# Finding the tokens of each expert from codes of four tokens, in an expert, attention, expert kernel on one core

## The chip, the cores and the metric

One core of a Trainium2 chip. The metric is the time of one execution on the device in microseconds, as the median of several runs. Engines are named as in the profile: PE is TensorE, DVE VectorE, ACT ScalarE, POOL GpSimd, SP the sync engine that issues most transfers.

## The reference

2,048 tokens of 256 values go through three residual stages: 0.5 of an expert layer, an attention layer, 0.5 of the same expert layer. All is float32.

```python
x = x + 0.5 * moe(layernorm(x))
x = x + attention(layernorm(x))       # 8 sequences of 256, 16 query heads, 4 key/value heads of 128
x = x + 0.5 * moe(layernorm(x))

def moe(x):                            # x: all T = 2048 tokens
    probs = softmax(x @ router_w.T)    # E = 64 experts
    wts, idx = top_k(probs, 8); wts = wts / sum(wts)
    order = argsort(idx.reshape(-1))   # by expert, within one by token
    pos = rank of the assignment within its expert
    valid = pos < 32                   # C = 32: an expert takes its first 32 tokens, the rest is dropped
    h = silu(x[tok] @ w1[e].T) * (x[tok] @ v1[e].T)     # F = 96
    out[tok] += (h @ w2[e]) * wts      # for valid assignments
```

The order of the tokens in an expert layer is position major: token number = 8 * position + sequence. So eight tokens that follow each other are one position of the eight sequences. With 16,384 assignments for 2,048 slots, most are dropped, and each expert keeps the 32 lowest token numbers that chose it.

## The kernel before, in words

**Expert layer** (twice, `expert_layer(0)` and `expert_layer(1)`, each engine has its part). x lies as 16 tiles of 128 tokens. DVE takes mean and variance (`bn_stats`, then `moments`, a row of small dependent operations called levels, each behind a semaphore wait) and writes the normalised tiles xn (L734). PE transposes them (L1139), multiplies with the router (L1117) and transposes back (L1128), ACT copies in between. For each four tiles DVE takes the eight largest logits (MAX8, L769), strikes them out (MATCH_REPLACE, L776) and writes the mask `chosen` (L778).

*Slots.* PE transposes the eight pairs of masks (L1158) into two banks, [expert and half, 512 tokens] each. DVE multiplies by `key_of_column` (L785), which falls with the token number, so that `keys` [128, 1,024] holds one half of the tokens for each expert in 64 partitions and the other half in the other 64. Four rounds of MAX8 (L789) and three of MATCH_REPLACE (L791) give the 32 largest keys, i.e. the lowest token numbers, of each half; both halves are copied side by side (L798, L799), and four more rounds on 64 columns (L801, L804) give the 32 of each expert. PE moves these to [slot, group of four experts] (L1165), DVE turns keys into `slot_index` (L809).

*Weights.* Between the first and second round DVE sums `exp8` and takes 0.5 over the sum (L795 to L797). POOL subtracts the largest logit (L464), ACT takes the exponential (L563), POOL scales (L468) and multiplies by the mask (L472).

*Table.* A table in device memory has one row of 320 values per token: 256 of xn, 64 weights. SP stores xn in eight transfers (L366) and the weights in two (L372). POOL then gathers 128 rows for each of 16 groups of four experts (L484), five in flight, after it has waited for `slot_ready` and for all ten stores:

```python
pool.wait_ge(slot_ready, slot_seen.add(2))
pool.wait_ge(table_written, written.add(160))
for g in range(GROUPS):
    if g >= IN_FLIGHT: ...
    nc.gpsimd.indirect_dma_start(out=slots[:, g % RING, :], ..., in_=table[:, :], ...)
```

*Slot steps* (17 per layer): PE transposes a gathered group (L1027), ACT copies, PE multiplies with the up weights (L1095), ACT and DVE form the gated product, PE transposes it (L1088) and multiplies with the down weights (L1105), ACT and DVE write the weighted result in two parts, and PE adds it into eight-sequence sums by one-hot marks (L1040, L1056).

**What orders the loads.** SP's program is written out by hand. Layer 0: x, small inputs, expert weights of groups 0 to 4 (1.25 MB each), two of the xn stores' four steps, group 5, the other two, groups 6 and 7, the weight stores, a wait for the first three gathers (L392), groups 8 to 11, then the attention weights `wk`, `wq`, `wv` after four slot steps, groups 12 to 15 into buffers as they come free, `wo`. Layer 1: groups 0 to 3 late in the attention; at `attention_done` groups 4 to 11 one behind the other, then the eight xn stores, then the weight stores.

**Attention**: four blocks of 512 tokens, 16 steps each, fp32 products as three fp32r products. DVE's `step` carries chores of block 0 (`in_step`), the late moments of tiles 4 to 15 in steps 8 and 9 among them; `moments(0, 4)` runs before the attention, `moments(0, 12)` before the last output, `moments(12, 16)` after it.

`keep_busy(n)` (L1064) issues n products of 128x128 in fp32 that nobody reads, each as two instructions in the profile.

## Time and profile before

| | us |
|---|---|
| median of 3 runs | 709.76 |
| lowest, highest | 708.30, 709.78 |
| the profiled execution | 710.26 |
| its span, first to last instruction | 708.4 |
| PE, DVE, ACT, POOL busy | 622.9, 509.8, 374.4, 53.8 |

Times in the rows are microseconds from the span's start unless a column says ns. Layer 0 lasts from 0 to about 105 us, the attention to about 606, layer 1 to the end. PE is busiest (88% of the span), but its busy time is no measure inside the expert layers, where it waits and runs at half clock for a part. In windows, PEclk is the granted clock of TensorE (1.00 is 2.4 GHz, 0.50 is 1.2 GHz) and the DMA share is the mean busy share of the core's 16 DMA engines, over 1 where packets overlap. An idle time in brackets names who ended it; "issue" stands for time in which the engine waited for nothing that the profile shows, a transfer's completion among it.

### The profile page before, as it was taken

The page shows a single profiled execution, that of the slowest core. Times are in us where ns is not written, and L with a number is a line of the kernel's source. Part 1 is how long each engine was busy: PE and PEld are TensorE (multiplying, and loading weights), DVE is VectorE, ACT ScalarE, POOL GpSimd, SP SyncE. Part 2 cuts the span into 40 slices and gives each one's busy share as a digit, 9 for nine tenths or more (in the row PEclk, how much of TensorE's full clock was granted, in tenths as well). Part 3 has the DMA queues.
Part 4 walks back from the last instruction along what each step waited for, and adds up shares of the span by engine and source line. Part 5 has one row for each costly group of instructions (what it writes and reads, how often), then busy time and mean ns, then how long its engine had stood idle before and what let it go on. Part 6 is the DMA issues. An engine that isn't in the chain of part 4 may idle for free.

```text
span 708.4 us, 12001 instructions
## 1 busy us (share of the span) xinstructions
PE 622.9 (88%) x4530; PEld 529.1 (75%) x4530; DVE 509.8 (72%) x1289; ACT 374.4 (53%) x1013; POOL 53.8 (8%) x57
## 2 busy tenths in 40 slices
PE   1729988899999999999999999999999998644995
PEld 1406667699988979999897999898799997422774
DVE  6665536688997777778777777876878776893442
ACT  1504534576756655656555656565566565421441
POOL 3153200000000000000000000000000000133310
PEclk9859989999999999999999999999999999875998
DMA  9949960000000000000000000000000042794571
GB/s 329 407 166 393 420 183 2 1 1 1 0 1 2 1 1 1 1 1 1 1 0 1 1 1 1 1 1 1 1 1 1 1 187 111 281 403 124 196 253 47
DMA packets 27133, 62.50 MB, mean 88 GB/s; under 512 B 6880, under 2 KB 17120, under 8 KB 26816
## 3 DMA queue, kind: packets, MB, share of 16 engines
q1 hardware_dynamic: 25008, 55.92, 21.0%
q0 software_dynamic: 1632, 5.38, 2.2%
q8 instruction: 38, 0.62, 0.4%
q10 hardware_dynamic: 432, 0.39, 0.2%
q14 instruction: 23, 0.19, 0.1%
HBM read 54.34 MB, written 7.34 MB: 87 GB/s over the span
## 4 chain that ended last, share of the span: by engine, by line
PE 77%; DVE 12%; DMA 5%; ACT 4%; issue 2%; SPq 0%; POOL 0%; DVEq 0%
PE bank L1214 18%; PE bank L1216 18%; PE bank L1215 18%; PE bank L1266 8%; PE bank L1056 3%; PE bank L1095 3%; DMA down_r<-down_in 3%; PE bank L1105 2%; PE bank L1027 1%; DVE best L789 1%; DVE ln L709 1%; PE bank L1040 1%; DVE keys L791 1%; PE bank L1139 1%; DMA x<-x_in 1%
## 5 line engine op out<-in xcount | busy, mean ns | idle before, releaser
L624 ACT ACTIVATE probs<-bank,negmax 128x256 f32<-128x256 f32 x256 | 121.4, 494 | 0.3 <-DVE negmax L939 0.3
L637 ACT CAST probsT_hi<-bank 128x512 fp32r<-128x512 f32 x128 | 68.9, 590 | 81.0 <-PE bank L1266 81.0
L971 DVE TENSOR_TENSOR probsT_lo<-bank,probsT_hi 128x512 fp32r<-128x512 f32 x128 | 82.0, 683 | 1.4 <-ACT probsT_hi L637 1.4
L939 DVE TENSOR_REDUCE negmax<-bank 128x2 f32<-128x512 f32 x128 | 82.0, 681 | 1.1 <-PE bank L1216 1.1
L607 ACT ACTIVATE o_hi<-bank,bv 128x512 fp32r<-128x512 f32 x64 | 44.2, 690 | 64.9 <-PE bank L1216 64.9
L1214 PE MATMUL bank<-k_hi,q_hi 128*128 128x256 f32 x256 | 72.6, 283 | 2.9 <-DVE q_lo L925 2.9
L947 DVE TENSOR_SCALAR probs<-probs,rowinv 128x256 f32<-128x256 f32 x256 | 73.1, 350 | 2.3
L1214 PE MATMUL bank<-o_hi,wo_hi 128*128 128x256 f32 x256 | 73.1, 286 | 1.6 <-DVE o_lo L925 1.6
L925 DVE SCALAR_TENSOR_TENSOR o_lo<-bank,bv,o_hi 128x512 fp32r<-128x512 f32 x64 | 48.0, 751 | 36.3 <-ACT o_hi L607 36.3
L1216 PE MATMUL bank<-o_hi,wo_lo 128*128 128x256 f32 x256 | 72.5, 283 | 0.0
L1216 PE MATMUL bank<-k_hi,q_lo 128*128 128x256 f32 x256 | 72.5, 283 | 0.0
L1215 PE MATMUL bank<-k_lo,q_hi 128*128 128x256 f32 x256 | 72.4, 283 | 0.0
L1215 PE MATMUL bank<-o_lo,wo_hi 128*128 128x256 f32 x256 | 72.2, 282 | 0.0
L925 DVE SCALAR_TENSOR_TENSOR q_lo<-bank,bq,q_hi 128x512 fp32r<-128x512 f32 x64 | 48.0, 749 | 28.4 <-ACT q_hi L607 28.2
L1266 PE MATMUL bank<-ident,probs 128*128 128x128 f32 x512 | 67.2, 275 | 0.6 <-DVE probs L947 0.6
L1266 PEld LDWEIGHTS bank<-ident,probs 128*128 128x128 f32 x512 | 58.1, 142 | 1.1 <-DVE probs L947 1.1
L624 ACT ACTIVATION_READ_ACCUMULATOR probs<-bank,negmax 128x1 f32 x256 | 57.4, 224 | 0.0
L1214 PE MATMUL bank<-probsT_hi,v_hi 128*128 128x512 f32 x128 | 51.5, 402 | 4.1 <-DVE xT_lo L923 3.2
L1214 PE MATMUL bank<-xT_hi,wq_hi 128*128 128x512 f32 x128 | 54.5, 426 | 0.2 <-DVE k_lo L925 0.2
L1214 PEld LDWEIGHTS bank<-k_hi,q_hi 128*128 128x128 f32 x256 | 48.8, 191 | 6.1 <-DVE q_lo L925 3.7
L607 ACT ACTIVATE q_hi<-bank,bq 128x512 fp32r<-128x512 f32 x64 | 44.8, 700 | 14.7 <-PE bank L1216 14.7
L1214 PEld LDWEIGHTS bank<-o_hi,wo_hi 128*128 128x128 f32 x256 | 48.3, 189 | 4.2 <-DVE o_lo L925 2.0
(165 smaller groups left out, 1318.1 us busy)
## 6 DMA issues: line engine op xcount, KB each, us to landing
up_r<-up_in SPq DMA_DIRECT2D x16, 768.0 KB, 9.3
down_r<-down_in SPq DMA_DIRECT2D x14, 512.0 KB, 10.1
up_q<-up_in SPq DMA_DIRECT2D x8, 768.0 KB, 8.2
up_o<-up_in SPq DMA_DIRECT2D x6, 768.0 KB, 11.9
down_q<-down_in SPq DMA_DIRECT2D x8, 512.0 KB, 9.0
token_table<-xn SPq DMA_DIRECT2D x16, 256.0 KB, 10.0
down_o<-down_in SPq DMA_DIRECT2D x6, 512.0 KB, 13.6
x<-x_in SPq DMA_DIRECT2D x4, 512.0 KB, 5.5
```

Source lines behind the costliest of these rows:

```text
L607: nc.scalar.activation(dst, src, ACT.Identity, bias=bias).then_inc(work_high, 1)
L624: nc.scalar.activation(probs[:, n % 2, t, :], scores_ps[head][:, qt * S:qt * S + S], ACT.Exp, bias=negmax[:, n % 2, t:t + 1], accum_out=ro ...
L637: nc.scalar.copy(probsT[0][:, head].rearrange("p c s -> p (c s)"), probsT_ps[head][:]).then_inc(probsT_high, 1)
L925: nc.vector.scalar_tensor_tensor(lo, src, bias, hi.bitcast(f32), ALU.add, ALU.subtract).then_inc(work_taken, 1)
L939: nc.vector.reduce_max(negmax[:, n % 2, 2 * head:2 * head + 2], scores_ps[head][:].rearrange("p (t s) -> p t s", t=2), AX.X, negate=True). ...
L947: last = nc.vector.tensor_scalar(probs[:, n % 2, t, :], probs[:, n % 2, t, :], rowinv[:, n % 2, t:t + 1], None, ALU.mult)
L971: nc.vector.tensor_tensor(probsT[1][:, head].rearrange("p c s -> p (c s)"), probsT_ps[head][:], probsT[0][:, head].rearrange("p c s -> p ( ...
L1056: last = mm(banks[n][:, D * pair:D * pair + D], marks[:, c:c + P], parts, start=start and pair == 0, stop=stop, skip_group_check=True)
L1214: mm(dst, w[0], m[0], start=start, stop=False, skip_group_check=shared)
L1215: mm(dst, w[0], m[1], start=False, stop=False, skip_group_check=shared)
L1216: return mm(dst, w[1], m[0], start=False, stop=stop, skip_group_check=shared)
L1266: last = nc.tensor.transpose(probsT_ps[head][:, c * S + qt * P:c * S + qt * P + P], probs[:, n % 2, 2 * head + qt, c * P:c * P + P], ident[:])
```

## The change

- **Codes.** ACT writes `code_ident`, four identity matrices scaled by 8, 4, 2, 1 over 32, four copies per expert layer. PE no longer transposes the masks but adds up four scaled transposes in one bank: [expert and half, 256 groups of four tokens], where the value is a code of four bits over 32. Half the partitions hold tokens 0 to 3 of each eight, the other half 4 to 7. DVE adds `key_of_group` to each non-zero code, searches 256 columns instead of 1,024 (`best`), splits rank and code, tests each bit (`part_bits`), gives each of the four tokens its key (`part_keys`), lays both halves side by side as 256 candidates per expert and searches those for the 32 largest.
- **Reciprocal column.** The table's row is 321 values: the 65th weight column is 0.5 over the sum, written by DVE ahead of the key search. POOL's scaling (L468) goes; DVE multiplies by the column in the slot step. POOL's subtraction waits for the masks now; SP's weight store waits for `winv_ready` too.
- **Moments.** 13 levels become 11: two Newton steps for the root in place of three, the first with other constants.
- **Unread products.** 24 on PE at the start, 12 ahead of layer 1, 16 after the move of the slot keys in each layer, ahead of the first gathered group's transposes.
- POOL's setup has six small iotas more, in each layer one iota and cast of 256 columns instead of 1,024.

```diff
-ROW = D + E
+ROW = D + E + 1
...
+KEPT = 0.375
...
+PARTS = B // 2
+GROUPS_OF_TOKENS = T // B
+CODES = 2 * 2 ** PARTS
...
-                chosen = sb(router, "chosen", [P, TILES // 2, 2, E])
-                expw = sb(router, "expw", [P, TILES, E])
+                chosen = sb(router, "chosen", [P, TILES // 2, 2, E], f32r)
+                expw = sb(router, "expw", [P, TILES, E + 1])
...
+                sp.wait_ge(winv_ready, inv_seen.add())
...
+            for n in range(PARTS):
+                nc.gpsimd.iota(bit_of_part[:, n:n + 1], pattern=[[0, 1]], base=2 ** (PARTS - 1 - n),
+                               channel_multiplier=0).then_inc(setup_link, 1)
+            for half in range(2):
+                pool.wait_ge(setup_link, 4 + PARTS + half)
+                nc.gpsimd.iota(part_offset[64 * half:64 * half + 64, :], pattern=[[2, PARTS]], base=2 * PARTS * half,
+                               channel_multiplier=0).then_inc(setup_link, 1)
+            pool.wait_ge(setup_link, 6 + PARTS)
...
-                for half in range(2):
-                    nc.gpsimd.iota(key_i32[64 * half:64 * half + 64, :], pattern=[[-1, 4], [-1024, 2], [-8, P]],
-                                    base=T - 4 * half, channel_multiplier=0).then_inc(key_raw, 1)
-                    pool.wait_ge(key_raw, raw.add())
-                nc.gpsimd.tensor_copy(key_of_column[:], key_i32[:]).then_inc(key_ready, 1)
+                nc.gpsimd.iota(key_i32[:, 0:GROUPS_OF_TOKENS], pattern=[[-2 * B, GROUPS_OF_TOKENS]], base=2 * T,
+                               channel_multiplier=0).then_inc(key_raw, 1)
+                pool.wait_ge(key_raw, raw.add())
+                nc.gpsimd.tensor_copy(key_of_group[:], key_i32[:, 0:GROUPS_OF_TOKENS]).then_inc(key_ready, 1)
 
                 pool.wait_ge(top8_ready, tops.add(4))
-                nc.gpsimd.tensor_tensor(expw[:], logits[:], top8[:, :, 0:1].to_broadcast([P, TILES, E]),
+                pool.wait_ge(chosen_ready, masks.add(4))
+                nc.gpsimd.tensor_tensor(expw[:, :, 0:E], logits[:], top8[:, :, 0:1].to_broadcast([P, TILES, E]),
                                         ALU.subtract).then_inc(shifted, 1)
                 pool.wait_ge(exps, exp_seen.add(2))
-                pool.wait_ge(winv_ready, inv.add())
-                nc.gpsimd.tensor_tensor(expw[:], expw[:], wsum[:, 1, :].unsqueeze(2).to_broadcast([P, TILES, E]),
-                                        ALU.mult).then_inc(scaled_ready, 1)
-                pool.wait_ge(chosen_ready, masks.add(4))
-                pool.wait_ge(scaled_ready, scales.add())
                 nc.gpsimd.tensor_tensor(
-                    expw[:].rearrange("p (h i) e -> p h i e", h=2), expw[:].rearrange("p (h i) e -> p h i e", h=2),
-                    chosen[:].rearrange("p i h e -> p h i e"), ALU.mult).then_inc(weights_ready, 1)
+                    expw[:, :, 0:E].rearrange("p (h i) e -> p h i e", h=2), expw[:, :, 0:E].rearrange("p (h i) e -> p h i e", h=2),
+                    chosen[:].bitcast(f32).rearrange("p i h e -> p h i e"), ALU.mult).then_inc(weights_ready, 1)
...
+                for n in range(PARTS):
+                    nc.scalar.activation(code_ident[:, n, :], ident[:], ACT.Copy,
+                                         scale=2.0 ** (PARTS - 1 - n) / CODES).then_inc(code_ready, 1)
...
-                          (tt, var, stats[:, a:b, 2], stats[:, a:b, 5], ALU.add)],
-                         [(stt, gap2, half_gap, 0.25, half_gap, ALU.mult, ALU.mult), (ts, var, var, 1.0 / D, EPS, ALU.mult, ALU.add),
-                          (ts, mean_, mean_, 0.5, None, ALU.mult)],
-                         [(tt, var, var, gap2, ALU.add)],
+                          (stt, var, stats[:, a:b, 2], EPS * D, stats[:, a:b, 5], ALU.add, ALU.add)],
+                         [(stt, gap2, half_gap, 0.25 / KEPT ** 2, half_gap, ALU.mult, ALU.mult), (ts, mean_, mean_, 0.5, None, ALU.mult)],
+                         [(stt, var, var, 1.0 / D / KEPT ** 2, gap2, ALU.mult, ALU.add)],
 
 
                          [(ts, rstd_.bitcast(i32), var.bitcast(i32), -0.5, ROOT_BITS, ALU.mult, ALU.add)]]
+
                 steps += [[(tt, gap2, rstd_, rstd_, ALU.mult)],
-                          [(stt, gap2, gap2, -0.5, var, ALU.mult, ALU.mult)],
-                          [(stt, rstd_, gap2, 1.5, rstd_, ALU.add, ALU.mult)]] * 3
+                          [(tt, gap2, gap2, var, ALU.mult)],
+                          [(stt, gap2, gap2, -10.0 / 3.0, gap2, ALU.add, ALU.mult)],
+                          [(stt, rstd_, gap2, 5.0, rstd_, ALU.add, ALU.mult)]]
+                steps += [[(tt, gap2, rstd_, rstd_, ALU.mult)],
+                          [(stt, gap2, gap2, -0.5 * KEPT ** 2, var, ALU.mult, ALU.mult)],
+                          [(stt, rstd_, gap2, 1.5, rstd_, ALU.add, ALU.mult)]]
...
-                    tie(nc.vector.tensor_tensor(weight4[:, parity, :], slots[:, u, s + D:ROW:GROUPS], quadrant[:], ALU.mult))
+                    tie(nc.vector.scalar_tensor_tensor(weight4[:, parity, :], slots[:, u, s + D:D + E:GROUPS], slots[:, u, D + E:ROW],
+                                                       quadrant[:], ALU.mult, ALU.mult))
...
+                dve.wait_ge(exps, 2 * layer + 1)
+                tie(nc.vector.tensor_reduce(wsum[:, 0, :], exp8[:], AX.X, ALU.add))
+                tie(nc.vector.reciprocal(wsum[:, 1, :], wsum[:, 0, :]))
+                nc.vector.tensor_scalar(expw[:, :, E], wsum[:, 1, :], 0.5, None, ALU.mult).then_inc(winv_ready, 1)
+
+
+
                 dve.wait_ge(key_ready, key_seen.add())
-                for n in range(2):
-                    dve.wait_ge(chosenT_raw, pairs_seen.add())
-                    last = nc.vector.tensor_tensor(keys[:, 512 * n:512 * n + 512], bank[n][:],
-                                                   key_of_column[:, 512 * n:512 * n + 512], ALU.mult)
-                tie(last)
+                dve.wait_ge(codes_raw, codes_seen.add())
+                codes = bank[0][:, 0:GROUPS_OF_TOKENS]
+                tie(nc.vector.scalar_tensor_tensor(keys[:], codes, 0.0, key_of_group[:], ALU.is_gt, ALU.mult))
+                tie(nc.vector.tensor_tensor(keys[:], keys[:], codes, ALU.add))
                 for n in range(C // 8):
                     tie(nc.vector.max(best[:, 8 * n:8 * n + 8], keys[:]))
                     if n < C // 8 - 1:
                         tie(nc.vector.match_replace(keys[:], best[:, 8 * n:8 * n + 8], keys[:], -1.0))
-                    if n == 0:
-
-                        dve.wait_ge(exps, 2 * layer + 1)
-                        tie(nc.vector.tensor_reduce(wsum[:, 0, :], exp8[:], AX.X, ALU.add))
-                        tie(nc.vector.reciprocal(wsum[:, 1, :], wsum[:, 0, :]))
-                        nc.vector.tensor_scalar(wsum[:, 1, :], wsum[:, 1, :], 0.5, None, ALU.mult).then_inc(winv_ready, 1)
-                nc.vector.tensor_copy(merged[:, 0:C], best[0:E, :])
-                tie(nc.vector.tensor_copy(merged[:, C:2 * C], best[E:P, :]))
+
+                nc.vector.tensor_copy(best_rank[:], best[:])
+                tie(nc.vector.tensor_scalar(best_code[:], best[:], float(CODES), None, ALU.mult))
+                nc.vector.tensor_tensor(part_bits[:], best_code[:].unsqueeze(2).to_broadcast([P, C, PARTS]),
+                                        bit_of_part[:].unsqueeze(1).to_broadcast([P, C, PARTS]), ALU.bitwise_and)
+                tie(nc.vector.tensor_tensor(part_keys[:], best_rank[:].unsqueeze(2).to_broadcast([P, C, PARTS]),
+                                            part_offset[:].unsqueeze(1).to_broadcast([P, C, PARTS]), ALU.subtract))
+                for half in range(2):
+                    rows = slice(E * half, E * half + E)
+                    last = nc.vector.scalar_tensor_tensor(merged[:, half], part_bits[rows], 0.0, part_keys[rows], ALU.is_gt, ALU.mult)
+                tie(last)
+                candidates = merged[:].rearrange("e h c n -> e (h c n)")
                 for n in range(C // 8):
-                    last = nc.vector.max(first_keys(n), merged[:])
+                    last = nc.vector.max(first_keys(n), candidates)
                     if n < C // 8 - 1:
                         tie(last)
-                        tie(nc.vector.match_replace(merged[:], first_keys(n), merged[:], -1.0))
+                        tie(nc.vector.match_replace(candidates, first_keys(n), candidates, -1.0))
...
-                    nc.vector.tensor_scalar(dst[:], bank[4][:, 0:GROUPS], -1.0, float(T), ALU.mult, ALU.add).then_inc(slot_ready, 1)
+                    nc.vector.tensor_scalar(dst[:], bank[4][:, 0:GROUPS], -0.5, float(T), ALU.mult, ALU.add).then_inc(slot_ready, 1)
...
+                pe.wait_ge(code_ready, PARTS * (layer + 1))
                 chosen_seen.add(2)
-                for n in range(2):
+                for m in range(2):
                     pe.wait_ge(chosen_ready, chosen_seen.add())
                     for c in range(4):
-                        last = nc.tensor.transpose(bank[n][:, c * P:c * P + P],
-                                                   chosen[:, 4 * n + c, :, :].rearrange("p h e -> p (h e)"), ident[:])
-                    last.then_inc(chosenT_raw, 1)
+                        part, h = 2 * m + c // 2, c % 2
+                        last = mm(bank[0][:, h * P:h * P + P], chosen[:, 4 * m + c, :, :].rearrange("p h e -> p (h e)"),
+                                  code_ident[:, part, :], start=part == h == 0, stop=part == PARTS - 1, skip_group_check=True)
+                last.then_inc(codes_raw, 1)
...
+                keep_busy(16)
...
+            for _ in range(24):
+                mm(bank[3][:, 0:P], ident[:], ident[:], start=True, stop=True)
...
+            keep_busy(12)
...
```

## Rows read from the trace of the kernel before

**Rows 1.** Chain that ended last, from 0 to 120 us: start, us, what.

```profile
45.78 0.35 PE bank L1165 x8
...
46.70 1.09 POOL slots L484
...
76.41 19.22 DMA down_r<-down_in
...
105.72 0.33 DVE ln L709 x3
...
108.59 1.39 DVE xn L912 x4
```

**Rows 2.** Windows, 56 to 90 us; last come PEclk, DMA share, GB/s.

```profile
56.00:90.00 34.00, 32.85 (x431) 23.37 (x423) 19.50 (x68) 18.73 (x57) 8.79 (x10) 1.00 1.02 416
```

**Rows 3.** Timeline of SyncE's queue, 0 to 110 us: start, us, engine, line.

```profile
41.65 1.34 SPq L372 DMA_DIRECT2D token_table<-expw  x2
52.32 0.33 SPq L357 DMA_DIRECT2D up_o<-up_in  x1
```

**Rows 4.** Chain that ended last, from 560 us on.

```profile
640.45 2.97 issue
```

**Rows 5.** Timeline of SyncE's queue, from 545 us on.

```profile
617.74 17.63 SPq L366 DMA_DIRECT2D token_table<-xn  x8
635.68 2.60 SPq L372 DMA_DIRECT2D token_table<-expw  x2
```

**Rows 6.** Windows, 40 to 41.5 us, columns as in rows 2.

```profile
40.00:41.00 1.00, 0.00 (x0) 0.00 (x0) 0.96 (x3) 0.00 (x0) 1.00 (x1) 0.50 0.12 47
41.00:41.50 0.50, 0.00 (x0) 0.00 (x0) 0.50 (x1) 0.00 (x0) 0.50 (x1) 0.50 0.06 25
```

**Rows 7.** Timeline of DVE, 9 to 58 us.

```profile
30.66 1.12 DVE L778 TENSOR_SCALAR chosen<-struck 128x256 f32<-128x256 f32 x1
...
33.72 1.23 DVE L789 MAX8 best<-keys 128x8 f32<-128x1024 f32 x1
...
35.06 1.21 DVE L791 MATCH_REPLACE8 keys<-best,keys 128x1024 f32<-128x1024 f32 x1
...
43.81 0.22 DVE L801 MAX8 slot_keys<-merged 64x8 f32<-64x64 f32 x1
```

**Rows 8.** Timelines of POOL and of ACT, 0 to 60 us.

```profile
29.61 2.03 POOL L464 TENSOR_TENSOR expw<-logits,top 128x1024 f32<-128x1024 f32 x1 [21.99 <-DVE top L769]
...
39.28 2.35 POOL L472 TENSOR_TENSOR expw<-expw,chosen 128x1024 f32<-128x1024 f32 x1
...
31.67 1.06 ACT L563 ACTIVATE expw<-expw 128x1024 f32<-128x1024 f32 x1 [1.48 <-POOL expw L464]
```

**Rows 9.** DMA, 42.8 to 45.6 us: rate in 40 slices, queue; weight stores' landing.

```profile
GB/s 0 11 154 267 285 293 282 293 285 293 293 293 285 293 286 278 289 293 285 293 282 293 285 293 293 293 285 271 128 22 0 0 0 0 0 0 0 0 0 0
...
q1 hardware_dynamic: 2080, 0.52, 82.8%
...
token_table<-expw SPq DMA_DIRECT2D x2, 256.0 KB, 2.8
```

**Rows 10.** Timeline of DVE, 595 to 656 us.

```profile
604.90 1.28 DVE L956 TENSOR_TENSOR x<-x,bank 128x512 f32<-128x512 f32 x2 [0.97 <-PE bank L1292]
```

**Rows 11.** DMA, 635.5 to 637.5 us: the queue, its packets, MB and share.

```profile
q1 hardware_dynamic: 799, 0.77, 109.4%
```

**Rows 12.** Chain that ended last, from 50 to 120 us.

```profile
51.82 1.44 PE bank L1095 x16
...
56.96 0.79 PE bank L1095 x16
...
113.03 1.50 PE bank L1064 x8
```

**Rows 13.** Timeline of PE, 0 to 54 us.

```profile
32.89 3.31 PE L1070 MATMUL bank<-x,ident 128*64 128x256 f32 x16
...
49.76 0.69 PE L1027 MATMUL bank<-ident,slots 128*128 128x128 f32 x2 [3.67 <-DMA slots<-token_table,slot_index]
```

31 lines of the change are left out of this document (17 added, 14 removed).

## The prediction

> **What bounds the kernel now.** I read the chain of waits first, cut at the two expert layers; between them TensorE carries it and the change touches little. In layer 0 the chain goes through the key search on DVE, which ends just before 45.78, through the gather at 46.70, and then into a transfer that was 19.22 us in the queue, `down_r`, landed at 95.63 [rows 1]. Next, the windows: from 56 to 90 us the DMA engines are busy 1.02 of the time at 416 GB/s [rows 2]. SyncE issues the loads of that stretch from 52.32 on, 5.62 behind the first gather, since it waits for the third to land [rows 3]. So layer 0 ends as early as its first gathers start, and no earlier for a faster TensorE or DVE in the slot steps.
>
> What does the first gather wait for? In layer 1 not for the keys: the slots were ready at 640.45, and 2.97 us of "issue" passed until GpSimd started at 643.42 [rows 4]. It also waits for the ten stores into the token table. SyncE issued the eight token stores over 17.63 us, held up by a full queue, and the two of the weights from 635.68 to 638.28 [rows 5]. This is a DMA backlog that begins with `attention_done`, and the change alters its bytes by four per row. **In layer 1 a shorter search is worth nothing.** In layer 0 the keys came last, but the same bound lies close ahead: the loads of groups 0 to 7 keep the engines full until about 39, and the tail of one or two engines reaches 41.45 (12% of the engines busy in 40 to 41, 6% in the next half microsecond) [rows 6].
>
> **Part 1, the search.** MAX8 takes 1.23 us on 1,024 columns and 0.22 on 64, MATCH_REPLACE 1.21 on 1,024 [rows 7]: 1.05 ns a column, so 0.42 and 0.40 on 256. A round is these two, a value load of 0.09 and the links: 0.97 against 2.58 now. The new timeline of layer 0: the moments give 0.5 (part 3). GpSimd's first product now waits for the masks, so it no more blocks the last of them, which took 1.12 at 30.66 and ended 0.14 behind GpSimd [rows 7, 8]; free, its 256 columns are 0.3 by the slope. It ends at 30.66 + 0.3 - 0.5 = 30.5. But now the scaling of the reciprocals, a tensor_scalar too, stands behind the same GpSimd operation (2.03): 32.7. Two key operations on 256 columns, 0.42 each with links: 33.6. Three rounds and a MAX8: 37.0. The split into parts is new: two short casts of 0.1 to 0.2, two operations of 128 and two of 128 columns on half the partitions, 0.29 each by the slope: 1.4, to 38.4. The second search is three rounds and a MAX8 again, 3.4 (with 64 columns 1.9): 41.8. To the gather it is 0.96, as from 45.74 to 46.70: **42.8 instead of 46.70**. The fp32r products of the codes replace transposes and run beside the sums of exp8: 0. They wait for four ACT copies of 128 columns, issued while ACT waits for TensorE: at worst 1 us on the keys, which 42.8 can bear (below). The short iota and cast on GpSimd lie 20 us ahead of their reader: 0.
>
> **Part 2, the weights.** GpSimd's product no longer needs the scaled one: 30.5 + 2.03, exp 1.06 [rows 8], product 2.35, with handovers 36.1. SyncE is free (its wait for `winv_ready` ends at 32.7), nothing else stands in its queue until the third gather, and the stores queue behind the loads. Alone, the two kept every engine busy for 82.8% of 2.8 us, 2.32 us for 2,080 packets, 18 ns for 256 B; the first bytes came at 42.9 and the second store landed 2.8 behind its issue at 42.99, at 45.8 [rows 3, 9]: 2.9 from first byte to landing. Behind the tail at 41.45 that makes 44.4, and with 0.3 for GpSimd (46.42 to 46.70) the gather goes at 44.7. That is later than 42.8: **the stores are late next**, and the gain is 46.70 - 44.7 = 2.0, not 3.9. The keys have 1.9 of slack.
>
> **Part 3, the moments.** Thirteen levels take 108.59 - 105.72 = 2.87, 0.2 each [rows 1]. Two levels and one operation less are 0.5. The call behind layer 0 pays in full: -0.5. The first call is covered by the backlog, and so is the last (four tiles); the one of twelve tiles ends ahead of DVE's idle 0.97 at 604.90 [rows 10]; the late moments in the attention are shorter by some 0.1 to 0.5 beside TensorE: 0, with -0.5 kept for the range.
>
> **Part 4, rows of 1,284 B.** Rows of 1,280 B start on multiples of 256 B, those of 1,284 do not. No row shows such a packet. Token packets kept the engines busy for 109.4% of 2 us at 799 packets, 44 ns on the mean and 46 for 1,024 B without the few tiny ones [rows 11]; against 18 for 256 B that is 9.3 ns for 256 B more. The lower bound is nothing, the upper one such piece for each packet: 128 packets per engine for the tokens and 128 for the weights, 1.2 us each, 2.4 per layer. I take 0.1 for the tokens, whose source stays as it was, and 0.3 for the weights, whose source and destination both shift: 0.4, near the rows of the same size. It counts in the backlog of either layer. The gathers read offset rows too, 8 per engine each; the 16 in layer 0 lie in the full stretch: +0.1 for all. The third operand in the slot weight: 0, DVE waits for ACT there.
>
> The Trainium skill, "DMA: Bandwidth & Descriptors", section "How a descriptor splits into AXI transactions", speaks against this change: a descriptor that starts off a 256 B boundary begins at the boundary below it, and the bytes ahead of its start cost beats all the same. By it the sum would be that of the first rival.
>
> **Part 5, extra matmuls.** The 24 at the start and the 12 ahead of layer 1 speed up only transposes whose gain the backlog covers: 0; should they end late, it is covered too. The 16 behind the keys: four calls took 1.50 [rows 12], so 6.0. In layer 0 they run from 42.2 to 48.2; the first slots can be taken 3.06 behind the gather [rows 13], at 48.2 with part 4: no delay, and what a warm clock saves there (sixteen matmuls in 1.44 cold, 0.79 warm [rows 12]) goes into the wait for `down_r`. In layer 1, where TensorE is the bound, they start some 4 us before 639.8 and end by 642, about five ahead of the slots; the clock stood at 0.50 in 40 to 41 [rows 6], after idle time since 36.2 [rows 13]. So the slot steps start cold as now: 0.
>
> **Sum** against the profiled execution: gather of layer 0 -2.0 + 0.4, gathers + 0.1, moments - 0.5, layer 1 + 0.4: **-1.6**. It took 710.26 us (span 708.4), 0.5 above the median of 709.76; from the median the forecast is **708.2**.
>
> **Rivals.**
> 1. *Half a piece for every packet.* 4.7 ns on 256 packets per engine, 1.2 per layer: -2.4 + 2.4 = 0.0, 709.8. For it: a packet's time follows its bytes in rows 9 and 11. Against it: nothing in the rows says that skipped bytes are moved. This is what the page's rule does here. Chance 0.26.
> 2. *Slower.* A whole piece or more for every packet, as each touches one block more and memory has to fill partly written blocks: 2.4 per layer, -2.4 + 4.8 = +2.4, 712.2. Its place is the gather of layer 1, which has no reserve: each microsecond of the stores is one of the kernel. It decides from 1.9 per layer. Against it: a 256 B packet pays only 8.7 above its share by bytes. Chance 0.14.
> 3. *The table doesn't bind*, since the tail vanishes and the gather of layer 0 goes by the keys at 42.8: -3.9 - 0.4 = -4.3, 705.5. Or the clock of layer 1 stays up over the gap, which with three cold steps warmed is 2 more than the forecast, 706.2. For it: the tail is one or two engines. Against it: the backlog of layer 1 had such a tail too, and the idle gap. Chance 0.15.
> 4. *The search isn't shorter*: integer operations or casts that cost twice as much, or a longer wait for GpSimd. Up to 1.9 us of that changes nothing, so it is part of the forecast.
>
> The forecast has 0.45. A measurement of this kernel tells 0.2%, 1.4 us, from no change. The forecast's own range is 0 to 0.7 per layer, -2.4 to -1.0, or 707.3 to 708.8; two thirds of it, and rival 3, are faster: 0.48. The rest of it and rival 1 are no change: 0.37. Slower 0.15. The range goes from 705.3, rival 3 with the late moments, to 711.2, and leaves out the full price of rival 2.
>
> **What would show it.** Right: in layer 0 the gather near 45 with the slots ready at about 42.5 and GpSimd idle between; the first loads 5.6 behind it and `down_r` landed 1.6 earlier; in layer 1 the gather 0.4 later behind `attention_done`, with "issue" of 6 us or more ahead of it; packets of the weights at 20 ns, of the tokens at 47. Wrong: a gather in layer 0 right behind the slot index; warm slot steps in layer 1 from the first; packets longer by 9 ns; or a search that lasts beyond 44.

## The result and the profile after

The changed kernel took **715.98 us** (median of 4 runs, 714.54 to 716.52) against 709.03 for the kernel before (707.47 to 709.78): a ratio of **1.0115, 95% interval [1.008, 1.015]**. It is slower by 7 to 8 us, where 708.2 had been predicted, and 715.98 lies far above the range. The profiled execution took 714.54, its span is 712.8.

The chain that ended last in layer 0 (start, us, what):

```profile
42.33 8.60 issue
50.93 1.07 POOL slots L495
...
80.78 19.84 DMA down_r<-down_in
```

And in layer 1, where `attention_done` came at 606.07 (606.29 in the profile of before):

```profile
636.11 12.22 issue
648.33 0.99 POOL slots L495
```

In both layers the slots are ready about 4 us earlier than before (42.33 against 46.42; 30.0 us behind `attention_done` against 34.2), and in both GpSimd starts the gather 4 to 5 us *later* (50.93 against 46.70 [rows 1]; 42.3 behind `attention_done` against 37.1 [rows 4]). "Issue" of 8.60 and 12.22 us stands where the kernel before had 0.3 and 2.97. The keys don't set the gather any more; the ten stores into the table do, and they have become slower. In layer 0 the wait passes on to `down_r`, landed at 100.62 instead of 95.63. That it isn't seen at `attention_done` has its cause between: from DVE's first `xT_lo` on, the attention took 490.2 us in this profile and 493.4 in that of before, near the two ends of what the profiles of all kernels show (490.1 to 493.6).

The search itself, DVE's timeline from 10 to 56 us (start, us, line, operation):

```profile
30.22 0.29 DVE L797 TENSOR_SCALAR chosen<-struck 128x256 fp32r<-128x256 f32 x1
...
31.03 1.61 DVE L804 TENSOR_SCALAR expw<-wsum 128x16 f32<-128x16 f32 x1
32.55 0.41 DVE L811 SCALAR_TENSOR_TENSOR keys<-bank,key_of_group 128x256 f32<-128x256 f32 x1
...
37.70 0.58 DVE L826 SCALAR_TENSOR_TENSOR merged<-part_bits,part_keys 64x128 f32<-64x128 int32 x2
...
42.15 0.17 DVE L838 TENSOR_SCALAR slot_index<-bank 128x16 uint32<-128x16 f32 x1
```

The stores, from POOL's timeline (the product that completes the weights) and from SyncE's queue in both layers:

```profile
33.77 2.16 POOL L483 TENSOR_TENSOR expw<-expw,chosen 128x1024 f32<-128x1024 f32 x1 [1.17 <-DMA token_table<-xn]
```

```profile
35.96 6.27 SPq L382 DMA_DIRECT2D token_table<-expw  x2
...
617.56 18.41 SPq L375 DMA_DIRECT2D token_table<-xn  x8
636.08 2.62 SPq L382 DMA_DIRECT2D token_table<-expw  x2
```

SyncE issues the weights at once, at 35.96, and nothing holds them back but the transfers ahead of them. What they are like on the DMA engines: 44 to 49 us, the rate in 40 slices and the queue (packets, MB, the time they took as a share of 16 engines):

```profile
GB/s 259 255 288 235 237 222 181 206 183 191 189 181 129 85 83 75 94 75 92 69 69 50 85 58 52 31 33 29 25 29 25 17 17 17 6 8 8 12 6 0
...
q1 hardware_dynamic: 1781, 0.49, 81.6%
```

81.6% of 16 engines for 5 us over 1,781 packets is **36.7 ns for 260 B**, where the same working of [rows 9] gave 18 ns for 256 B. Hardly anything else is moving: the packets are slow by themselves. And they are uneven: 30 ns from 44 to 46 us (1,331 packets, 124.5%), 56 ns from 46 to 49 (450 packets, 52.9%). The rate of [rows 9] is a plateau of 290 GB/s that ends within 0.2 us, here it fades over three microseconds, while GpSimd waits for the last of them. The tokens' packets have the same trouble. From 637 to 640 us (the view and columns as before):

```profile
q1 hardware_dynamic: 935, 0.77, 113.5%
```

That is 58 ns a packet on a mean size of 0.77 MB over 935, some 820 B, against 44 for larger ones in [rows 11]. In a stretch with few small ones, 635 to 636 us, it is 51 ns (347 packets, 110.1%), and from 638 to 639 us 68 ns (259, 110.8%). The weights' packets behind them, 640 to 647 us, take 46 ns on the mean (1,966, 80.0%), more than in layer 0.

TensorE's clock in layer 1, in windows (length, busy time of PE, PEld, DVE, ACT, POOL; then PEclk, DMA share, GB/s):

```profile
640.00:642.00 2.00, 1.54 (x14) 1.35 (x13) 0.00 (x0) 0.00 (x0) 0.00 (x0) 1.00 1.28 158
642.00:644.00 2.00, 0.00 (x0) 0.00 (x0) 0.00 (x0) 0.00 (x0) 0.00 (x0) 1.00 1.23 91
644.00:646.00 2.00, 0.00 (x0) 0.00 (x0) 0.00 (x0) 0.00 (x0) 0.00 (x0) 1.00 0.25 21
646.00:648.00 2.00, 0.00 (x0) 0.00 (x0) 0.00 (x0) 0.00 (x0) 0.00 (x0) 0.69 0.04 2
648.00:650.00 2.00, 0.00 (x0) 0.00 (x0) 0.00 (x0) 0.00 (x0) 1.37 (x2) 0.50 0.00 0
```

The unread products end in 640 to 642; TensorE idles from there, and the granted clock is back at 0.50 before the first gather has landed.

### The profile page after: what moved, and what is told of

Read it like the earlier page. It is cut to its first block, busy times and chain, and to the rows that moved or that the text cites. A ratio compares the mean times of both kernels' runs of the same rounds, so it can differ in the third digit from the quotient of the medians.

```text
span 712.8 us, 12276 instructions
## 1 busy us (share of the span) xinstructions
PE 637.2 (89%) x4666; PEld 543.8 (76%) x4666; DVE 502.7 (71%) x1282; ACT 375.7 (53%) x1021; POOL 45.5 (6%) x59
## 4 chain that ended last, share of the span: by engine, by line
PE 73%; DVE 10%; DMA 5%; ACT 5%; issue 4%; POOL 1%; SPq 1%; DVEq 0%; ACTq 0%
PE bank L1248 18%; PE bank L1249 17%; PE bank L1250 17%; PE bank L1300 7%; PE bank L1085 3%; DMA down_r<-down_in 3%; PE bank L1124 3%; PE bank L1134 2%; DMA slots<-token_table,slot_index 2%; PE bank L1069 1%; PE bank L1056 1%; DMA x<-x_in 1%; PE bank L1168 1%; PE bank L1146 1%; POOL slots L495 1%
```

## The experiments

Fifteen kernels ran, in four batches (e1 to e4, e5 to e8, e9 to e12, e13 to e15), each beside 21 to 29 runs of the kernel before, whose medians there were 706.8 to 707.4 us. For each, three times that carry the argument are read from its trace: the gather of layer 0; the gather of layer 1 behind `attention_done` (in brackets the slot index, behind the same event); and the rest, from that gather to the end of the span. Each kernel ran 4 to 12 times; the rows "before" and "after" are those of the first comparison, and each row's three times come from one profile.

| kernel | row, B | ratio to before [95%] | gather 0 | gather 1 (slots 1) | rest |
|---|---|---|---|---|---|
| before | 1,280 | 1 | 46.70 | 37.1 (34.2) | 65.0 |
| after | 1,284 | 1.0115 [1.008, 1.015] | 50.93 | 42.3 (30.0) | 64.5 |
| e1 before, wide row | 1,284 | 1.0182 [1.0142, 1.0223] | 51.26 | 42.2 (34.7) | 65.3 |
| e2 codes, no column | 1,280 | 0.9994 [0.9974, 1.0013] | 45.67 | 37.3 (31.1) | 65.2 |
| e13 e2, shifted source | 1,280 | 0.9982 [0.996, 1.0003] | 45.83 | 37.1 (30.9) | 65.4 |
| e3 | 1,344 | 1.0012 [0.9998, 1.0026] | 46.52 | 38.3 (30.0) | 66.0 |
| e4 | 1,312 | 1.0026 [1.0, 1.0052] | 46.51 | 38.9 (30.0) | 66.8 |
| e12 | 1,296 | 1.0013 [0.9993, 1.0032] | 47.64 | 39.2 (30.0) | 64.3 |
| e14 | 1,288 | 1.0093 [1.0064, 1.0122] | 48.78 | 41.0 (30.0) | 65.1 |
| e5 before, stores earlier | 1,280 | 1.0005 [0.9973, 1.0037] | 46.51 | 34.4 (34.2) | 67.7 |
| e10 e5, loads held | 1,280 | 0.9992 [0.9973, 1.0011] | 46.36 | 34.9 (34.7) | 65.0 |
| e6 e2, stores earlier | 1,280 | 0.9898 [0.9857, 0.994] | 46.12 | 31.8 (31.1) | 67.2 |
| e7 e6, layer 0 too | 1,280 | 0.9902 [0.9875, 0.993] | 44.64 | 32.1 (31.1) | 65.5 |
| e8 e7, no unread products | 1,280 | 0.9928 [0.99, 0.9956] | 44.04 | 32.0 (31.7) | 67.9 |
| **e9 e7, loads held** | 1,280 | **0.9873 [0.9848, 0.9899]** | 43.51 | 32.0 (31.1) | 64.0 |
| e11 after, as e9 | 1,284 | 1.0027 [1.0011, 1.0042] | 49.31 | 37.3 (30.0) | 65.0 |
| e15 e12, as e9 | 1,296 | 0.9946 [0.9926, 0.9965] | 44.58 | 34.1 (30.0) | 68.0 |

**Is it the row?** e1 is the kernel before with nothing but a column of zeros behind the weights, which nobody uses:

```diff
-ROW = D + E
+ROW = D + E + 1
...
+                nc.gpsimd.memset(expw[:, :, E:E + 1], 0.0).then_inc(key_raw, 1)
```

> The kernel before with one column more in the table's row (zeros, stored and gathered, read by nobody): rows of 1,284 B, weight packets of 260 B, all else as before. Theory (the offset rows make the stores slow): layer 1's gather starts 5 us later behind attention_done than before's 37.1, weight packets take 30 to 45 ns on the mean and token packets 55 to 70, and the whole is 714 to 718 us. Rival A (the cost of the change lies in its other parts: codes, split, unread products): the gather stays where it was and the time is 709 to 710.

It measured 1.0182 [1.0142, 1.0223], 718.81 us: the slowest kernel of all, and just above the 714 to 718 I had named. Its chain in layer 1:

```profile
643.67 7.48 issue
651.15 1.02 POOL slots L486
```

The gather is 5.1 us later than in the kernel before, as expected. Token packets take 52 ns from 638 to 639 us (344 packets, 111.5%) and 65 from 640 to 641 (277, 112.5%). Weight packets take 35 ns in layer 0 (44.5 to 50 us: 1,698, 67.3%) and 48 in layer 1 (643 to 650: 2,019, 85.9%), the latter above the 45 that I had named.

e2 is the other half of that test, the whole change without the column (GpSimd's scaling is back):

```diff
-ROW = D + E + 1
+ROW = D + E
...
+                pool.wait_ge(winv_ready, inv.add())
+                nc.gpsimd.tensor_tensor(expw[:], expw[:], wsum[:, 1, :].unsqueeze(2).to_broadcast([P, TILES, E]),
+                                        ALU.mult).then_inc(scaled_ready, 1)
```

> The changed kernel with the reciprocal column alone undone: rows of 1,280 B again, GpSimd scales by the reciprocals again (1.9 us more ahead of the weight stores); codes, moments, unread products stay. Theory: layer 1's gather at 37 behind attention_done, layer 0's at 44.5 to 46, packets of 18 and 46 ns, 706 to 709.5 us. Rival A: 714 to 716, little changed.

It measured 0.9994 [0.9974, 1.0013]; its chain at the gathers of both layers:

```profile
42.06 3.61 issue
45.67 1.09 POOL slots L500
...
633.00 6.17 issue
639.16 1.00 POOL slots L500
```

So the column carries the whole loss, 1.0115 over 0.9994 or **1.2%, 8.6 us** (in the kernel before 1.8%; why it is more there isn't shown), and everything else in the change together is worth nothing that can be told from zero. The two traces split it: layer 0's gather is 5.3 us later with the column, of which 4.2 are left at `attention_done`; layer 1's is 5.0 later; behind it 0.8 come back; in sum 8.4, the difference of the spans, 712.8 - 704.4.

**Which offsets?** e3, e4, e12 and e14 are the changed kernel with columns of zeros behind the reciprocal one, up to 80, 72, 68 and 66 in all, which GpSimd sets early; in e3 and e4 `held_token` lies in the place of `slot_weight`, to make room:

```diff
-ROW = D + E + 1
+WIDTH = 80
+ROW = D + WIDTH
```

> The changed kernel with 15 zeros behind the reciprocal column: rows of 1,344 B, that is 21 times 64 B but off the 256 B grid in three of four rows, weight packets of 320 B. Theory, if what costs is a partly written piece of 64 B or less: token packets back at 46 ns, weights at 20 to 21, layer 1's gather 37.5 behind attention_done, 706.5 to 710 us. Rival B (any start off a 256 B boundary costs): token packets stay at 53 ns or more, 712 to 716 us.

> As the one of 1,344 B with 7 zeros: rows of 1,312 B, 41 times 32 B, weight packets of 288 B. If the piece is 32 B: packets at 46 and 20 ns and 706.5 to 710 us as with 1,344. If it is 64 B: half of the rows are written in part, packets between those of 1,344 and of 1,284, 710 to 714 us. If 256 B: 712 to 716.

> The changed kernel with three columns of zeros behind the reciprocal column: rows of 1,296 B, which start on multiples of 16 B but not of 32, and weight packets of 272 B. Rows of 1,312 B (multiples of 32) gave 1.0026 with the gather of layer 1 at 38.9 us behind attention_done, rows of 1,284 B gave 1.0115 with 42.3. Theory (memory is written in units of 32 B and a part of one costs): as 1,284, the gather at 41 to 42.5 and the ratio at 1.009 to 1.012. Rival (the unit is 16 B or less, what hurts are offsets of 4 B): as 1,312, the gather at 38.5 to 39.5 and the ratio at 1.002 to 1.004.

> The changed kernel with one column of zeros behind the reciprocal column: rows of 1,288 B, on multiples of 8 B. Rows of 1,284 B gave the gather of layer 1 at 42.3 us behind attention_done, those of 1,296 B 39.2. Theory (the unit is 16 B): as 1,284, gather at 41.5 to 43, ratio 1.009 to 1.013. Rival (only odd multiples of 4 B cost): as 1,296, gather at 38.5 to 39.5, ratio 1.001 to 1.004.

"Issue" ahead of layer 1's gather was 8.27 us in e3, 9.20 in e12 and 10.93 in e14 (12.22 with 1,284 B). Against e2 the gather of layer 1 is later by 1.0 us with rows of 1,344 B, 1.5 with 1,312, 1.9 with 1,296, 3.7 with 1,288 and 5.0 with 1,284, although the wider rows carry more bytes. In layer 0 it is 0.9, 0.8, 2.0, 3.1 and 5.3. By the ratios, rows that are multiples of 16 B cost 0.2 to 0.3% or less, and those of 8 or 4 B 1%. My expectation of one unit of 32 B failed in e12, that of 16 B holds by e14's ratio, but its gather came at 41.0, below the 41.5 that I had named: what holds is that the finer the offset, the dearer.

The packets show two steps in this. The next table has mean times in stretches of layer 1, worked out as above, of one microsecond where only a start is given: one in which almost only token packets move (1,024 B, the same source in every kernel), and one in which almost only weight packets do.

| row, B | token packets, ns | weight packets, ns |
|---|---|---|
| 1,280 (e2) | 44 (from 632) | 17 (from 635, 256 B) |
| 1,344 (e3) | 49 (631 to 636) | 27 (from 638, 320 B) |
| 1,312 (e4) | 51 (from 635) | 29 (from 639, 288 B) |
| 1,296 (e12) | 51 (from 632) | 29 (from 637, 272 B) |
| 1,288 (e14) | 51 (from 635) | 27 (from 638), 51 (from 640, 264 B) |
| 1,284 (after) | 51 (from 635), 68 (from 638) | 52 (from 642, 260 B) |

Each of the five lengths that aren't a multiple of 256 B costs 5 to 7 ns per token packet and 10 to 12 per weight packet. So the packets that I expected of e3 and of e4, 46 and 20 to 21 ns, were wrong, though both times (707.92 and 709.22 us) lie in the range named. Rows on multiples of 8 and of 4 B are dearer on top of that, and the later in the stream the more.

The Trainium skill ("DMA: Bandwidth & Descriptors", "How a descriptor splits into AXI transactions") charges a descriptor that starts off a multiple of 256 B for the bytes below its start. By that rule rows of 1,296 and of 1,288 B pay about alike, since both spread their starts over all of 256 B. The trace agrees in kind for the first step (token packets of 51 ns in both) and not for the second: the runs have 1.9 and 3.7 us at the gather, and 5.0 for 1,284, where half a piece for each packet would be 1.2.

**Source or destination?** e13 is e2 with the weights 260 B apart in SBUF, of which 256 B are stored into rows of 1,280 B:

```diff
-                expw = sb(router, "expw", [P, TILES, E])
+                expw = sb(router, "expw", [P, TILES, E + 1])
...
-                                 expw[:, half:TILES:2, :]).then_inc(table_written, 16)
+                                 expw[:, half:TILES:2, 0:E]).then_inc(table_written, 16)
```

> The kernel with codes and without the reciprocal column (rows of 1,280 B), in which the weights lie 260 B apart in SBUF and 256 B of each are stored: the source of the weight stores is shifted, the row in device memory is not. Theory (the row in device memory makes the packets long): as without the shift, weight packets of 256 B at 16 to 19 ns on the mean, the gather of layer 1 at 37.0 to 37.8 us behind attention_done, ratio 0.999. Rival (the shifted source does it): weight packets of 25 ns or more on the mean, the gather 1 us or more later, ratio 1.002 or more.

0.9982 [0.996, 1.0003], both gathers as in e2: the shifted source costs nothing; what costs is on the side of device memory. For the tokens it is the row's start alone, since their packets (1,024 B) and their source are the same in e2 and in the changed kernel. For the weights the start and the length changed together (260 B in place of 256), and no run separates the two. Its DMA view of 40 to 44.6 us has one thing more:

```profile
GB/s 301 410 319 327 214 356 252 361 256 365 247 334 292 325 252 321 305 309 167 158 98 38 18 53 25 38 36 36 38 36 36 36 36 36 38 36 36 31 18 18
```

Full speed to 42.1, then, but for a dip, 36 GB/s up to 44.4. [Rows 9] have 293 for 16 engines, so this is the rate of two of them at their normal pace. That they were last with the loads and had their share of the weights still ahead is my reading; no view names the engines.

Reading the shifted rows is free as well: the first gather that the chain waits for in layer 1 took as long from rows of 1,284 B as from those of 1,280:

```profile
649.63 2.94 DMA slots<-token_table,slot_index
```

(after), and in e10:

```profile
636.99 2.85 DMA slots<-token_table,slot_index
```

In e2, with rows of 1,280 B too, it took 2.94.

**Is a shorter search worth anything once the stores are early?** In layer 1 e5 moves them ahead of most loads, in the kernel before; e6 does the same to e2, and e7 moves layer 0's weight stores ahead of the load of group 7 too:

```diff
-            for g in range(len(homes_q), AHEAD):
+            for g in range(4, 6):
                 load(1, g)
             for n in range(4):
                 store_tokens(n)
+            for g in range(6, 10):
+                load(1, g)
             store_weights()
+            for g in range(10, AHEAD):
+                load(1, g)
```

> The kernel before; only SyncE's order in layer 1 changes: at attention_done two groups' weights, then the token stores, four groups, the weight stores, the last two groups. Theory (layer 1's gather waits for the stores behind 10 MB of loads, 3 us longer than for the keys): the gather starts right behind the slot index, about 34 us behind attention_done instead of 37.1, 2.5 to 3 us less in all, ratio 0.996. Rival C (it is no backlog but the latency of the stores or the waits of SyncE): the gather stays at 37 behind attention_done, ratio 1.0.

> The codes without the column (as e2) with the same order in layer 1. Theory: now the search counts in layer 1: slots ready at 31 behind attention_done, the gather at 31 to 32, so 5 to 6.5 us less than e2 and about 3 us less than e5's gather; ratio to before 0.990 to 0.994. Rival C: as e2, ratio 0.999.

> As e6, and in layer 0 the weight stores go ahead of the loads of group 7. Theory: layer 0's gather at 42.5 to 43.5 instead of 45.7; the stretch of loads behind it begins and ends 2 to 3 us earlier, and if nothing in the attention takes it up the ratio falls by 0.003 to 0.004 against e6. Rival D (layer 0's end is taken up in the attention, as the changed kernel's attention_done was not later though its gather of layer 0 was 4 us later): attention_done stays and the ratio is e6's.

e5 missed. The gather came at 34.4, 0.3 behind the slots, just as hoped, and the rest gave all of it back. TensorE's waits of e5 from 636 to 650 us (engine, line, waited for: us in total, times, longest), and a window of it:

```profile
PE bank L1031 <- DMA slots<-token_table,slot_index: 6.6, 1, 6.6
```

```profile
642.00:644.00 2.00, 0.00 (x0) 0.00 (x0) 0.00 (x0) 0.00 (x0) 1.45 (x2) 0.50 1.04 431
```

The first gather shares the engines with the loads of groups 10 and 11, which now stand behind the weight stores: 431 GB/s while TensorE waits 6.6 us for 128 rows. In the kernel before the engines moved 3 GB/s from 642 to 644 us.

With the short search the same move pays: e6 0.9898 [0.9857, 0.994], e7 0.9902 [0.9875, 0.993]. Layer 1's gather is at 31.8 to 32.1, within a microsecond of the slots. The 1% between e5 and e6 is that of the codes, the moments and the unread products together; without these products (e8, below) it is 0.8%. Layer 0's gather, 1.5 us earlier in e7 than in e6 but behind the 42.5 to 43.5 expected, isn't seen in the time, nor at `attention_done` (602.38 against 601.89).

e8 is e7 without the unread products (24, 12 and twice 16):

```diff
-                keep_busy(16)
...
-            for _ in range(24):
-                mm(bank[3][:, 0:P], ident[:], ident[:], start=True, stop=True)
...
-            keep_busy(12)
```

> As e7 without the 24, 12 and 16 unread products. Theory: the 16 end some 5 us or less ahead of the slots now that the gather comes early, so they may keep the clock: without them layer 1's first slot steps are at half clock, 1 to 2 us more than e7. If they did nothing, the same as e7 within 0.1%.

0.9928 [0.99, 0.9956]; the intervals of e7 and e8 overlap, so the ratios don't settle it. The traces show what happened in that place. The window 640 to 642 us of e7, then of e8:

```profile
640.00:642.00 2.00, 1.03 (x12) 0.62 (x16) 0.85 (x3) 0.52 (x2) 1.12 (x2) 1.00 0.81 282
```

```profile
640.00:642.00 2.00, 0.98 (x4) 0.58 (x4) 0.85 (x3) 0.37 (x1) 1.17 (x2) 0.50 0.87 287
```

The first sixteen matmuls with the up weights took 0.83 us in e7 and 1.44 in e8, and the rest 65.5 and 67.9. But the products don't do this reliably. e6 has the same program as e7 in layer 1, products included, and its rest was 67.2:

```profile
641.00:645.00 4.00, 3.78 (x42) 2.08 (x46) 1.34 (x6) 1.26 (x4) 1.06 (x2) 0.68 0.18 54
```

In e6 the clock rose while more of the products were left, so they ended at 637.9 us, and TensorE then waited 1.5 and 1.4 us for the first two gathers (0.8 and 0.7 in e7). The granted clock was 0.61 in 642 to 644 and 0.53 in 644 to 646, where e7 has 1.00. So one comparison of profiles has 2.4 us for the products and the other 0.7, and what they are worth in the median isn't shown.

**Does the collision explain the miss?** e9, e10 and e11 hold the two loads until layer 1's first three gathers have landed; e9 is e7, e10 is e5, and e11 is the changed kernel with rows of 1,284 B and both orders.

```diff
             store_weights()
+            for n in range(3):
+                sp.wait_ge(gathered[n], 16 * 4)
             for g in range(10, AHEAD):
                 load(1, g)
```

> The kernel with codes but without the reciprocal column (rows of 1,280 B), with the orders of both layers moved, and now the loads of groups 10 and 11 of layer 1 held until the first three gathers have landed, so that they no more collide with them. Theory (collision): gather of layer 1 stays at 32 to 32.5 us behind attention_done, the stretch from that gather to the end of the span falls from 65.5 to about 64, and the ratio to the kernel before is 0.987 to 0.989 (0.990 without the hold). Rival (the two loads are needed soon, or the collision was no longer the bound once TensorE was warm): the stretch stays at 65 to 66 and the ratio at 0.990 or above; in that case TensorE's waits for the weights of group 10 show it.

> The kernel before, with the stores of layer 1 moved ahead as in the order tried before, and the loads of groups 10 and 11 held until the first three gathers have landed. That order alone brought the gather of layer 1 from 37.1 to 34.4 us behind attention_done and gave the 2.7 back between gather and end (67.66 against 64.98). Theory (what gave it back was the collision of two loads with the first gathers): gather at 34.4, the rest back at 65.0 to 65.3, ratio 0.9965. Rival (it was given back by cold slot steps or by something else behind the gather): the rest stays at 67 or more and the ratio is 1.000.

> The changed kernel as it is, with rows of 1,284 B, with both orders moved and the two loads held. It differs from the first kernel of this batch by the reciprocal column alone. Theory A (each store packet into rows of 1,284 B takes longer by itself, 37 against 18 ns for the weights, and about 18 more for the tokens): 128 packets of each kind per engine make some 4.5 us in layer 1 wherever the stores lie, so its gather comes at 36 to 37 us behind attention_done and the ratio is 0.994 to 0.996. Rival B (the long packets come from the end of a backlog, when nothing else runs beside them and each waits for itself): with loads queued beside and behind the stores the engines stay full, the gather comes at 32 to 33.5 and the ratio is at most 0.990.

e9 has the lowest median of the study: **698.36 us, 0.9873 [0.9848, 0.9899]**; its interval overlaps those of e6 and e7. Its gather in layer 1 follows the slots almost at once:

```profile
632.63 0.85 issue
633.49 0.99 POOL slots L506
```

and the rest is 64.0, as expected, against 65.5 in e7. That the hold did it isn't shown: e6 and e7 differ by 1.7 with the same program there. In e10 the rest went back from 67.7 to 65.0 as expected, and TensorE's wait for the first gather from 6.6 to

```profile
638.69 0.69 PE L1033 MATMUL bank<-ident,slots 128*128 128x128 f32 x2 [3.60 <-DMA slots<-token_table,slot_index]
```

3.6 us (PE's timeline). But 0.9992 [0.9973, 1.0011] doesn't show the 0.35% that this should bring; 0.9973 is the nearest it comes. Runs of one kernel spread by some 0.4% to either side of their median here (before in that batch: 704.32 to 710.28), and the profile of e10 is its fastest run. That the collision was the cause in e5 is shown by its trace, not by its time.

e11 settles the packets. It differs from e9 by the column alone. The queue of e11 in 634.2 to 640.4 us, when the weights are stored:

```profile
q1 hardware_dynamic: 2207, 0.98, 76.6%
```

and of e9 in 628.5 to 632.1:

```profile
q1 hardware_dynamic: 2125, 0.65, 69.0%
```

34.4 ns against 18.7 on the mean. Both stretches hold the last packets of the loads too (102 and 31 of more than 2 KB); nearly without them it is 29.6 ns from 636 to 638 us (1,188 packets, 109.8%) against 16.5 from 629.5 to 631.5 (1,409, 72.5%). So the packets are long wherever the stores stand. The gather is 5.8 us later in layer 0 and 5.4 in layer 1, the kernel by 1.0027 over 0.9873, 1.6% or 11 us. Theory A was right in kind, and both its sizes were too small (36 to 37 expected, 37.3 measured; 0.994 to 0.996 expected, 1.0027 measured).

**Is the column worth having in rows of a good length?** e15 is e9 with the column, in rows of 1,296 B.

> The changed kernel with rows of 1,296 B, both orders moved and the two loads held. It differs from the best kernel so far (0.9873, gathers at 43.5 and at 32.0 behind attention_done) by the reciprocal column and 16 B per row. Theory (the column is worth nothing, as the stores of the weights are not late by GpSimd but by the queue): gathers 0.5 to 1.5 later in each layer, ratio 0.988 to 0.991. Rival (GpSimd's scaling of 2 us was in the way once the queue is not): gathers earlier than 43.5 and 32.0, ratio below 0.986.

0.9946 [0.9926, 0.9965]: no. It is 0.7% behind e9, more than I expected. The slots come 1.1 us earlier than in e9 and the gathers 1.1 and 2.1 later. The wait that opens ahead of the gather in layer 1, 4.09 us, also lets the clock fall. Windows of e15:

```profile
636.00:638.00 2.00, 0.88 (x9) 0.69 (x7) 0.05 (x1) 0.00 (x0) 1.47 (x2) 1.00 0.44 110
638.00:640.00 2.00, 1.11 (x8) 0.56 (x12) 0.86 (x3) 0.37 (x1) 1.42 (x2) 0.83 0.49 143
640.00:642.00 2.00, 2.00 (x19) 0.89 (x19) 0.00 (x0) 0.37 (x1) 1.67 (x2) 0.50 0.54 111
```

The unread products end in 636 to 638, TensorE is idle for 45% of the next window, and the slot steps run at half clock, where e9 has 1.00 in the windows from 636 on. The rest is 68.0 against 64.0. The clock can't be all of it, since kernels whose slot steps start at half clock too have 64.3 to 65.4 (e12, e2, e13). The chain of e15 has something that the chain of no other kernel has in layer 1:

```profile
640.38 2.97 another core or an unknown queue
643.37 0.26 ACT gate L540
```

ACT's first `gate` waits 2.97 us for something that the profile doesn't name, and TensorE waits 1.8 us for what follows from it. Whether this comes in every execution isn't known; the profiled one, 704.71 us, is among the slowest of twelve with a median of 703.24. So the 0.7% is measured, and its cause is in part open.

## Why the prediction was wrong, step by step

**Part 4 failed, and by its size.** It took 0.4 us per layer for the rows of 1,284 B, within 0 and 2.4. The column costs 5.3 us at the gather of layer 0 and 5.0 at that of layer 1 (after against e2), over twelve times the value and twice the upper bound. The step in which it went wrong is "one such piece for each packet": the bound was the price of moving 256 B more (9.3 ns), and the weights' packets grew by 19 ns, from 18 to 36.7. "For the tokens, whose source stays as it was" 0.1 was taken; but the source doesn't matter (e13), the row in memory does, and the tokens' rows shift as much as the weights'. And the bound was a mean: GpSimd waits for the last packet, and the rate's long fade shows how far it lies behind. For rows on multiples of 16 B or more the bound would have held: 0.8 to 2.0 us later at the gathers of either layer. The rest came with the offsets of 4 B.

**Rival 2 was right in its sign and its place**: a whole piece or more for each packet, decisive from 1.9 us per layer, at the gather of layer 1 that has no reserve. It had 0.14, and its price was half of what came. Its reason, that memory has to fill partly written blocks, fits the runs: stores suffer and gathers don't, the destination matters and the source doesn't, and the finest offsets cost most. But no run looks into the memory, so that stays an explanation and is not shown. The argument against it, "a 256 B packet pays only 8.7 above its share by bytes", came from rows in which every row started on a multiple of 256 B, and so had nothing to say on shifted ones. Rival 1 (half a piece) fell with it.

**Part 1 was right.** The last mask took 0.29 and DVE's scaling stood behind GpSimd's subtraction as foreseen (31.03 to 32.64, expected 32.7); the slots were ready at 42.33, expected "about 42.5". That a shorter search is worth nothing in layer 1 is what e2 shows: slots 3.0 us earlier, gather at 37.3 against 37.1. Rival 4 didn't come up.

**Part 2 was right in kind.** GpSimd was done at 35.93 (expected 36.1), and the stores were late next. Without the column the gather went at 45.67 instead of the 44.7 expected: the tail of two engines, which in e13 lasts to 44.6, was put 1.0 too short. So the change without its column should have brought 2.5 us by my own terms (-2.0 and -0.5), 0.35%; e2 and e13 show 0.06% and 0.18%, with 0.9974 and 0.996 as their lower ends: the parts that held are worth at most about this, and perhaps nothing. (The two spans, 704.4 and 708.4, differ by more, since the profile of before lies at the slow end of that kernel's runs.) Rival 3 (the table doesn't bind) is refuted in both kernels.

**Part 3** was right to 0.1 us: the moments behind the start and behind `attention_done` are 0.4 to 0.5 shorter each. **Part 5** held too: in layer 0 the unread products delayed nothing, in layer 1 the slot steps started cold in the changed kernel. What I had not worked out is the other side: with the stores early and the search short they can keep the clock up, as in e7 and e9 and not in e6.

**The chances** were added up wrongly. By the terms given, faster is two thirds of 0.45 and 0.15, that is 0.45 and not 0.48, and no change 0.41 and not 0.37. The range and the forecast don't hang on it.

## What to carry to other kernels

Before a table's row gets a column, price the row's length as the writer sees it: four bytes more on 1,280 doubled the mean time of the small stores here, and the same column in rows on multiples of 16 B cost a fifth to two fifths of that at the gather, and was still not worth the 2 us of GpSimd that it saved. When a chain that ends in several arms is shortened, look at which arm is next and move its *place in the queue* first: the short search, with the moments and the unread products, was worth 0 as it stood and 1% once SyncE's stores were moved ahead of loads that nobody needed soon. And a move that frees a transfer early lets others start early; e5's gain at the gather was gone by the end, as two loads met the first gathers. Holding them brought TensorE's wait and the rest back, but no gain that the times of e10 show.

## What was unexpected of the hardware

- Stores into device memory whose rows are 1,284 B apart take 30 ns per 260 B at first and 56 in the last three microseconds, 36.7 on the mean (layer 0; 46 in layer 1), against 18 ns per 256 B into rows of 1,280 B, with little else on the engines in either case. Token packets of 1,024 B take 51 and later 68 ns against 44. The shift of the source in SBUF is free (e13), and so is reading such rows (2.94 against 2.85 and 2.94 us for a gather).
- The cost has two steps. Each of the five row lengths off a multiple of 256 B made token packets 5 to 7 ns longer and the small ones 10 to 12; multiples of 8 and of 4 B cost more on top. At the gather of layer 1 that is 1.0, 1.5, 1.9, 3.7 and 5.0 us for 1,344, 1,312, 1,296, 1,288 and 1,284 B.
- The granted clock outlasts the work of TensorE for a while: in the changed kernel it was 1.00 in the windows up to 646 us, with no matmul after 642, and 0.50 from 648 on. Behind the unread products it stayed at 1.00 over TensorE's waits of 0.8 and 0.7 us (e7) and fell after waits of 1.5 and 1.4 (e6) and of 1.1 and 0.9 (e15).
- A gather of 128 rows that meets two loads took TensorE 6.6 us of waiting instead of 3.6 (e5, e10).
